# Attention block in one core: values copied by ScalarE without their bias, queries split by VectorE in another double step, and projections of values and outputs placed behind the values' products

## What is computed

```python
x = x + layernorm(attn(layernorm(x)))        # B, S, D, H, HD = 2, 2048, 128, 16, 64
x = x + layernorm(ffn(layernorm(x)))

def attn(x, Wq, bq, Wk, bk, Wv, bv, Wo, bo):
    q = einsum('bsd,dhk->bshk', x, Wq) + bq
    k = einsum('bsd,dhk->bshk', x, Wk) + bk
    v = einsum('bsd,dhk->bshk', x, Wv) + bv
    p = softmax(einsum('bqhd,bkhd->bhqk', q / sqrt(64), k))
    return einsum('bqhd,hdm->bqm', einsum('bhqk,bkhd->bqhd', p, v), Wo) + bo
```

## Time and profile before

| | |
|---|---|
| median of 3 runs | 2389.18 us (2385.74 to 2389.94) |
| profiled execution, time | 2388.58 us |
| profiled execution, span | 2386.7 us |
| mean granted TensorE clock over the span | 0.992 |
| PE busy | 98% of the span |
| DVE busy | 2035.4 us, 85% |
| POOL busy | 2107.2 us, 88% |
| ACT busy | 1415.4 us, 59% |
| DMA | mean 26 GB/s |

### The profile page before, as it was taken

The page is one execution under the profiler, slowest core; times in us unless marked ns, Lnnn a source line. Parts: engine busy times, 40 slices in busy tenths (PEclk is TensorE's granted clock), DMA queues, the critical chain, the costliest instruction groups (busy, mean ns, idle before and its releaser), DMA issues.

```text
span 2386.7 us, 43553 instructions
## 1 busy us (share of the span) xinstructions
PE 2348.6 (98%) x15628; PEld 1178.0 (49%) x15628; DVE 2035.4 (85%) x3208; ACT 1415.4 (59%) x1671; POOL 2107.2 (88%) x1206
## 2 busy tenths in 40 slices
PE   6999999999999999999999999999999999999998
PEld 3455454545445454454545445454544545444454
DVE  7888888888888888888888888888888888888877
ACT  5656556566565656656565655656656565655646
POOL 5888989888898989989888898989989888899986
PEclk8999999999999999999999999999999999999999
DMA  1100001000000000100001000100000000110101
GB/s 51 29 14 28 28 15 33 28 15 28 28 20 28 28 15 28 34 15 27 28 16 32 28 19 23 33 23 20 28 27 20 28 28 15 35 30 21 37 27 36
DMA packets 62969, 62.55 MB, mean 26 GB/s; under 512 B 28868, under 2 KB 46660, under 8 KB 62756
## 3 DMA queue, kind: packets, MB, share of 16 engines
q1 hardware_dynamic: 61748, 59.44, 8.5%
q10 hardware_dynamic: 1008, 0.33, 0.1%
HBM read 56.88 MB, written 2.61 MB: 25 GB/s over the span
## 4 chain that ended last, share of the span: by engine, by line
PE 94%; DVE 2%; POOL 1%; DMA 1%; ACT 1%; issue 1%; SPq 0%; POOLq 0%; DVEq 0%; ACTq 0%
PE o_ps L442 37%; PE spare_ps L401 14%; PE score_ps L421 10%; PE score_ps L427 10%; PE score_ps L424 10%; PE spare_ps L387 3%; PE spare_ps L487 3%; PE spare_ps L378 3%; PE spare_ps L369 3%; PE spare_ps L454 1%; DVE max_part L867 1%; POOL total L1142 1%; DMA m_all<-m_scratch 0%; DVE ln_stats L835 0%; PE spare_ps L467 0%
## 5 line engine op out<-in xcount | busy, mean ns | idle before, releaser
L1142 POOL TENSOR_TENSOR total<-total,probs 128x832 f32<-128x832 f32 (+1 forms) x896 | 1761.0, 1965 | 232.6 <-ACT probs L691 161.1
L867 DVE TENSOR_REDUCE max_part<-spare_ps 128x1 f32<-128x512 f32 x2027 | 1303.6, 685 | 295.3 <-PE spare_ps L401 276.7
L691 ACT ACTIVATE probs<-score_ps 128x1024 f32<-128x1024 f32 x1024 | 999.2, 1021 | 785.4 <-PE score_ps L427 784.2
L442 PE MATMUL o_ps<-probs,v_sb 128*64 128x512 f32 x4096 | 977.2, 598 | 0.0
L442 PEld LDWEIGHTS o_ps<-probs,v_sb 128*64 128x64 f32 x4096 | 268.3, 136 | 434.7 <-issue 282.5
L401 PE MATMUL spare_ps<-k_hi,q_hi 64*128 64x512 f32 x2027 | 466.2, 454 | 6.9 <-DVE max_part L867 3.2
L401 PEld LDWEIGHTS spare_ps<-k_hi,q_hi 64*128 64x128 f32 x2027 | 195.2, 184 | 436.8 <-issue 262.1
L421 PE MATMUL score_ps<-q_hi,kd_hi 64*128 64x512 f32 x2048 | 406.9, 393 | 0.9 <-ACT score_ps L681 0.9
L427 PE MATMUL score_ps<-q_hi,kd_lo 64*128 64x512 f32 x2048 | 405.2, 392 | 0.0
L424 PE MATMUL score_ps<-q_lo,kd_hi 64*128 64x512 f32 x2048 | 403.8, 390 | 0.0
L903 DVE TENSOR_REDUCE part_sum<-probs 128x192 f32<-128x768 f32 (+1 forms) x255 | 392.4, 1539 | 0.8 <-ACT probs L691 0.7
(11 more groups left out here) (136 smaller groups left out, 1118.5 us busy)
## 6 DMA issues: line engine op xcount, KB each, us to landing
m_all<-m_scratch SPq DMA_DIRECT2D x64, 512.0 KB, 4.4
denom<-denom_scratch SPq DMA_DIRECT2D x122, 128.0 KB, 2.9
m_scratch<-neg_rows SPq DMA_DIRECT2D x256, 1.0 KB
y_acc<-in_L_attn_x SPq DMA_DIRECT2D x8, 256.0 KB, 6.6
key_f<-in_L_attn_x SPq DMA_DIRECT2D x8, 256.0 KB, 2.8
block_out<-probs SPq DMA_DIRECT2D x8, 256.0 KB, 2.3
denom_col<-denom SPq DMA_DIRECT2D x61, 4.0 KB
denom_scratch<-denom_col SPq DMA_DIRECT2D x61, 4.0 KB, 1.4
```

The source lines that it names most:

```text
L442: last = nc.tensor.matmul(o_ps[half(h), :], v_sb[:, b, kt, half(h)], probs[:, st % RING, h, :], start=(kt == 0), stop=(kt == T - 1))
L691: nc.scalar.activation(probs[:, st % RING], score_ps[st % 2][:], ACT.Exp, scale=SCALE).then_inc(s["exp_done"], 1)
L867: nc.vector.reduce_max(max_part[:, G % 2, h, qt, kc:kc + 1], bank[max_bank(n, h)], AX.X).then_inc(s["max_done"], 1)
L1142: nc.gpsimd.tensor_tensor(others(total[:, G % 2], G), so_far, others(probs[:, st % RING], G), ALU.add).then_inc(s["sum_done"], 1)
```

## The change

The copy of the values moves from VectorE to ScalarE and loses its bias (`act_v`). The bias goes into the output's bias before the loop: `pool_bias` multiplies all of Wo with bv and folds the eight pairs together, `bias` lets TensorE sum over the rows at n = 3, and `dve_bias` adds that to `bo`. V runs in four groups of four tiles at d = 5 of every quarter. Q runs at d = 7, one quarter earlier than before counted in quarters (G + 3 instead of G + 2), and VectorE makes both of its parts. On TensorE V and Wo stand behind the values' products; Q and K stay ahead of them. On VectorE the output's addition stands behind the partial sums.

```diff
-V_AT = {(0, 7): (0, 2), (1, 7): (2, 2), (2, 4): (4, 2), (2, 7): (6, 2), (3, 0): (8, 3), (3, 4): (11, 3), (3, 7): (14, 2)}
+V_AT = {(0, 5): (0, 4), (1, 5): (4, 4), (2, 5): (8, 4), (3, 5): (12, 4)}
-Q_AT, M_OUT_AT, M_BACK_AT = 2, 4, 5
+Q_AT, M_OUT_AT, M_BACK_AT = 7, 4, 5
+def queries_at(n):
+    if n == 2:
+        return 2
+    G = n // PER_CHUNK + 3
+    return G if n % PER_CHUNK == Q_AT and G < CHUNKS else None
+BIAS_AT = 3
-FIRST_V_AT = {(2, 7): (0, 4), (3, 0): (4, 4), (3, 4): (8, 4), (3, 7): (12, 4)}
+FIRST_V_AT = {(1, 5): (0, 4), (2, 5): (4, 4), (3, 4): (8, 4), (3, 6): (12, 4)}
+            def bias(self):
+                self.pe.wait_ge(s["bias_scaled"], 4)
+                ps = self.take(SPARE["bias",], "bias", 0)
+                for k in range(2):
+                    last = nc.tensor.matmul(ps[half(k), 0:D], ones[:], bias_rows[:, 0, :], start=True, stop=True)
+                last.then_inc(s["bias_ps"], 1)
 # TensorE's loop
                 if keys_at(u, c, d):
                     me.project_k(*keys_at(u, c, d))
-                if values_at(u, c, d):
-                    me.project_v(*values_at(u, c, d))
-                if d == Q_AT and G + 2 < CHUNKS:
-                    me.project_q(G + 2)
-                if projected_at(G, d) is not None:
-                    me.out_projection(projected_at(G, d))
+                if queries_at(n):
+                    me.project_q(queries_at(n))
...
                     me.values(2 * n - 2)
                     me.values(2 * n - 1)
+                if values_at(u, c, d):
+                    me.project_v(*values_at(u, c, d))
+                if projected_at(G, d) is not None:
+                    me.out_projection(projected_at(G, d))
 # ScalarE
+        def act_v(act, u, t0, nt, name=None):
+            at = u * T + t0
+            act.wait_ge(s["v_ps"], at + nt)
...
+            nc.scalar.activation(v_sb[:, u % B, t0:t0 + nt, :].rearrange("p t n -> p (t n)"), bank[name or SPARE["V", at]][:, 0:nt * P],
+                                 ACT.Copy).then_inc(s["v_done"], nt)
...
                     act_seed(act, 2 * n + 3)
+                if values_at(u, c, d):
+                    act_v(act, *values_at(u, c, d))
                 if keys_at(u, c, d):
                     act_k(act, *keys_at(u, c, d))
...
-                if d == Q_AT and G + 2 < CHUNKS:
-                    act_q(act, G + 2)
 # VectorE
         def dve_q(dve, G, name=None):
             ps = bank[name or SPARE["Q", G]]
+            dve.wait_ge(s["q_ps"], G + 1)
...
+            nc.vector.tensor_scalar(q_hi[:, G % Q_RING, :], ps, b_qk[:, G // (B * NC) % 2, 0:1], None, ALU.add).then_inc(s["q_hi_done"], 1)
             dve.wait_ge(s["q_hi_done"], G + 1)
...
-                if values_at(u, c, d):
-                    dve_v(dve, *values_at(u, c, d))
-                if projected_at(G, d) is not None:
-                    dve_y(dve, projected_at(G, d))
...
                     dve_merge(dve, G - 1)
+                if projected_at(G, d) is not None:
+                    dve_y(dve, projected_at(G, d))
 # GpSimd, once before the loop
+        def pool_bias(pool):
+            pool.wait_ge(s["bias_in"], 32)
+            nc.gpsimd.tensor_tensor(bias_rows, bias_rows, b_v[:].unsqueeze(2).to_broadcast([P, PAIRS, D]), ALU.mult).then_inc(s["bias_scaled"], 1)
+            for k, count in enumerate((4, 2, 1)):
...
```

More of the change, by code:

```diff
@@ L133, in spare_banks @@
             use("V", v * T + t0)
-        if d == Q_AT and G + 2 < CHUNKS:
-            use("Q", G + 2)
+        if queries_at(n):
+            use("Q", queries_at(n))
         if projected_at(G, d) is not None:
             use("Wo", projected_at(G, d))
+        if n == BIAS_AT:
+            use("bias")
         if n in HEADS_AT:
@@ L170, in build @@
     bk_v = bk.rearrange("(i h) k -> i (h k)", h=2)
-    bv_v = bv.rearrange("(i h) k -> i (h k)", h=2)
+    bv_v = bv.rearrange("(i h) k -> (h k) i", h=2)
+    wo_rows = Wo.rearrange("(i h) k m -> (h k) i m", h=2)
     ctx = ExitStack()
@@ L186, in build @@
         b_qk = sb("b_qk", [P, 2, 2])
[L187 removed]
+        b_v = sb("b_v", [P, PAIRS])
         w_o = sb("w_o", [P, 2, D])
@@ L350, in take @@
                     pe.wait_ge(s["exp_done"], k + 1)
+                elif was == "bias":
+                    pe.wait_ge(s["bias_done"], 1)
                 elif was == "U":
@@ L581, in pe_program @@
                     me.project_k(*keys_at(u, c, d))
-                if values_at(u, c, d):
-                    me.project_v(*values_at(u, c, d))
-                if d == Q_AT and G + 2 < CHUNKS:
-                    me.project_q(G + 2)
-                if projected_at(G, d) is not None:
-                    me.out_projection(projected_at(G, d))
+                if queries_at(n):
+                    me.project_q(queries_at(n))
                 if n in HEADS_AT:
                     me.head_projections(HEADS_AT[n])
+                if n == BIAS_AT:
+                    me.bias()
                 if n == CENTRE_AT:
@@ L661, in act_k_high @@
             nc.scalar.activation(kd_hi[:, u % B, c * CH:(c + 1) * CH], key_diff[:], ACT.Copy).then_inc(s["kd_hi_done"], 1)
+        def act_v(act, u, t0, nt, name=None):
+            at = u * T + t0
+            act.wait_ge(s["v_ps"], at + nt)
+            if u >= 2 and t0 == 0:
+                act.wait_ge(s["pv_done"], (u - 1) * NC * T)
+            nc.scalar.activation(v_sb[:, u % B, t0:t0 + nt, :].rearrange("p t n -> p (t n)"), bank[name or SPARE["V", at]][:, 0:nt * P],
+                                 ACT.Copy).then_inc(s["v_done"], nt)
         def act_q(act, G, name=None):
@@ L773, in act_program @@
             act_x(act, 4)
+            act_v(act, 0, 0, TC, FIRST_V_BANK)
             act_x(act, 5)
@@ L851, in dve_x_statistics, with dve_bias @@
             statistics(dve, [y_acc[:, g * TC + t, :] for t in range(TC)], g, s["stats_done"], s["mv_done"], g)
[L853 to L860, removed]
+        def dve_bias(dve):
+            dve.wait_ge(s["bo_in"], 16)
+            dve.wait_ge(s["bias_ps"], 1)
+            nc.vector.tensor_tensor(bo_sb[:], bank[SPARE["bias",]][:, 0:D], bo_sb[:], ALU.add).then_inc(s["bias_done"], 1)
         def dve_max(dve, n, h):
@@ L1083, in dve_program @@
                     dve_merge(dve, G - 1)
+                if projected_at(G, d) is not None:
+                    dve_y(dve, projected_at(G, d))
                 if keys_at(u, c, d):
                     dve_k(dve, *keys_at(u, c, d))
-                if d == Q_AT and G + 2 < CHUNKS:
-                    dve_q(dve, G + 2)
+                if queries_at(n):
+                    dve_q(dve, queries_at(n))
                 if n in HEADS_AT:
@@ L1244, in pool_program @@
             first_rstd(7)
+            pool_bias(pool)
             for n in range(DOUBLES):
@@ L1316, in sp_denom_back @@
                 sp.wait_ge(s["o_norm_done"], G - 1)
+            elif G == 0:
+                sp.wait_ge(s["bias_ps"], 1)
             for h in range(2):
```

23 lines of the change are left out of this document (14 added, 9 removed).

## The result

| | before | after |
|---|---|---|
| median | 2386.57 us (20 runs, 2384.91 to 2389.94) | 2391.18 us (20 runs, 2390.02 to 2392.83) |
| profiled execution, span | 2386.7 us | 2389.9 us |
| granted TensorE clock | 0.992 | 0.993 |
| PE, DVE, ACT, POOL busy | 98%, 85%, 59%, 88% | 98%, 86%, 59%, 88% |

The ratio is 1.0017, 95% interval 1.0011 to 1.0023: the changed kernel is 0.17% slower, inside the 0.2% that was called no change. The time forecast was 2391, worked out from a median before of 2389.18 over three runs; over twenty runs that median is 2386.57. The change forecast was +2.3 us; the change measured is +4.6.

What follows compares the result with a forecast made beforehand. TensorE, busy 98%, was taken as the bound. +2.4 us steady and one-time terms made +2.3 on the profiled 2388.58, so 2390.9, forecast as 2391 with the median 0.6 above; range 2377 to 2404, chance 0.44 of staying within 4.8 us.

Steps and rivals of the forecast that it cites:

- +2.4 in the steady part: Sum of the quarter's terms, +0.04 us a quarter, over some 60 quarters.
- -0.1 once: One-time terms outside the steady quarters: bias matmuls 0.2 us, and -0.3 for VectorE's dropped first copy of values.
- d = 5 and 6: V's move to d = 5 costs 0 within 0.02; d = 6 loses its 0.12 us from late VectorE.
- d = 7: Q ahead of the products still waits 0.16 us for VectorE, where V waited 0.15.
- d = 2: VectorE starts pair A's reductions 0.85 late after the output's addition; costs 0.06 us, between 0 and 0.12.
- d = 3: The merge makes VectorE reduce pair A 0.88 late; costs 0.09 us, between 0 and 0.12.
- Placing V and Wo behind the products: At d = 5 and d = 1 on TensorE: V's place priced at 0, moving Wo gains nothing.
- rival 2: Slower: output's addition bounds d = 2, from a delay of 0.95; 18 us, 2409; chance 0.28 including its half.
- rival 1: Faster: VectorE on time at d = 7, 2372, chance 0.12; only d = 2 and 3 free, 2382, chance 0.16.
- All that the change can win in the steady part: TensorE's loss to late VectorE at d = 6 and 7: about 0.27 us a quarter, 17 us in 64 quarters.
- The bias's matmuls: One-time cost of TensorE's four passes of 128 columns for the folded bias: 0.2 us.
- The start, -0.3: VectorE's first copy of values leaves a stretch where TensorE waits for it: between 0 and -0.7 us.

Runs made afterwards that it cites:

- experiment 6: Changed kernel with V and Wo back ahead of the products, nothing else: 2390.22 us, ratio 1.0012.
- Experiment 4: Changed kernel with the output's addition back ahead of the partial sum and the merge on VectorE, Wo still behind the products: 2474.94 us.
- experiment 10: Changed kernel, V at d = 7, Q at d = 2 with ScalarE's Q part first, n = 2 banks in TensorE's order, `v_split` at n = 480: 2382.34 us.
- experiments 1 and 2: First: kernel before with V in fours at d = 5, 2403.82 us; second: changed kernel with Q at d = 2, high part on ScalarE, 2408.82 us.
- experiment 3: Changed kernel with the spare banks of n = 2 handed out in TensorE's order, Q before V: 2390.92 us, ratio 1.0016.
- Experiment 9: Changed kernel with n = 2 banks in TensorE's order and VectorE's `v_split` made at n = 480: 2388.96 us, ratio 1.0005.
- experiment 8: Changed kernel with n = 2 banks in TensorE's order and the last Q at n = 486 instead of 487: 2390.75 us, ratio 1.0013.
- experiment 1: Kernel before with V in groups of four at d = 5, still copied by VectorE and ahead of the products: 2403.82 us, ratio 1.0072.
- experiment 5: Changed kernel with n = 2 banks in TensorE's order, V at d = 7, Q at d = 2 with high part on ScalarE: 2387.57 us, ratio 1.0002.

## Why the prediction was right, and where it was wrong

**The time was right in part by chance.** Forecast were +2.4 in the steady part and -0.1 once, on a base of 2389.18. The base was 2.6 too high and the change by the medians, +4.6, twice what was forecast; the two errors cancel to the 2391. The profile shows +0.11 a unit, which is +0.03 a quarter for the +0.04 forecast and 1.4 us in units 1 to 13, and +1.7 at the ends. The steady part bears the forecast out, though in part by luck as well: d = 6 gave 0.04 less and d = 2 cost 0.06 less than forecast, and these cancel. The ends don't: they held two things that the prediction hadn't looked for.

**d = 5 and 6** (0 and -0.12): right in kind. 4.79 and 3.92 us. In this quarter d = 6 gave the 0.12; on the mean of a unit it was 4.00 before, because of the 3.97 in the third quarter, and gave 0.08.

**d = 7** (Q waits 0.16): right. 4.96 is 3.92 + 0.88 + 0.16. VectorE's first operation for Q has a pitch of 0.77 (1260.86 to 1261.63), where 0.66 was taken between 0.60 and 0.75: above the upper bound by 0.02, and covered as forecast, since the next pair A is still reduced 0.54 behind TensorE (1262.89 in the same timeline, against 1262.35). The Trainium skill, "VectorE: DVE Perf Modes", section on the TRN2 errata, gives an estimate of 0.66; the 62 operations here have a mean duration of 0.74.

**d = 2** (0.06, between 0 and 0.12): the term was mis-sized, it is 0. TensorE's timeline and VectorE's at d = 1 to 3 of a quarter after:

```profile
1232.31 0.39 PE L419 MATMUL spare_ps<-k_hi,q_hi 64*128 64x512 f32 x2
1232.63 1.94 PE L460 MATMUL o_ps<-probs,v_sb 128*64 128x512 f32 x8
1234.40 1.04 PE L505 MATMUL spare_ps<-w_o,o_sb 128*64 128x128 f32 x16
1235.37 0.50 PE L419 MATMUL spare_ps<-k_hi,q_hi 64*128 64x512 f32 x2
...
1239.31 0.51 PE L419 MATMUL spare_ps<-k_hi,q_hi 64*128 64x512 f32 x2
```

```profile
1233.95 1.52 DVE L938 TENSOR_REDUCE part_sum<-probs 128x192 f32<-128x768 f32 x1
1235.49 0.69 DVE L981 TENSOR_TENSOR y_acc<-spare_ps,y_acc 128x512 f32<-128x512 f32 x1
1236.10 1.28 DVE L898 TENSOR_REDUCE max_part<-spare_ps 128x1 f32<-128x512 f32 x2
...
1238.76 1.51 DVE L947 TENSOR_REDUCE total<-part_sum 128x192 f32<-128x768 f32 x1
1240.20 2.65 DVE L898 TENSOR_REDUCE max_part<-spare_ps 128x1 f32<-128x512 f32 x4
```

The addition starts 1.09 behind Wo, 0.04 sooner than K's copy starts behind K, and Wo starts 2.09 behind pair B where 2.18 was taken. Both together bring VectorE to 0.73 behind pair A where 0.85 was forecast. So much is early enough: experiment 6 has 0.60 and the same time. **d = 3** (0.09): right, 0.10, with VectorE 0.89 behind pair A. The Trainium skill's rule that weight loads are pulled ahead of running matmuls ("TensorE: Matmul & The Clock Gate", "Step-by-step: what each phase is for") would have made this free; the trace shows a price of 0.10 at 0.89 and none at 0.73.

**Placing V and Wo behind the products** (nothing, either way): right by experiment 6. Experiment 4 shows that this holds because the addition moved with Wo: with the addition back in its old place rival 2's mechanism comes about, and costs 84 us.

**The rivals.** Half of rival 1's cheaper form came true, d = 2 free; the other half, d = 3, didn't, and Q's wait stayed. Rival 2's delay of 0.95 at d = 2 was not reached (0.73).

**"All that the change can win in the steady part", 17 us:** the sum didn't rest on this step, and no run won that much: the best, experiment 10, won 0.30 a unit, under 5 us. What the step left out is that time at d = 7 also covers the seeds, with a margin of 0.21. V's wait of 0.15 fits into that margin; the 0.50 that V's tiles take at d = 7 doesn't. The waits before showed nothing of this, for the margin was still positive. The expectations of experiments 1 and 2 carried the omission further: they took d = 7 to 4.02, were forecast faster, and lost 0.40 to 0.45 at d = 0.

**Once.** The bias's matmuls, 0.2: right, n = 3 takes 4.15 for 3.92. The start, -0.3: -0.85, but this can't be credited to the change. Ahead of the loop and into n = 0, TensorE was granted the lower clock for 20.5 us in the profile before and for 13.7 in the one after; experiment 6, whose program is the changed kernel's up to there, shows 20.5 us and starts the loop 0.7 later than it. No run shows the term by itself. Not foreseen: +1.8 at n = 2 by the order in which banks are handed out, shown by experiment 3, and +2.0 at n = 488. Experiment 9 shows that this hangs on the wait behind the split; why the clock falls after it in some kernels and not in others is open. n = 0 gave back 0.7, which goes with the clock too (4.61 us after, 5.53 in experiment 6), and in the last unit one Q fewer gave back 0.75 and other places 0.3. The first unit holds that Q instead; n = 8 and 16, together 0.9 shorter, made up for it.

## What to carry to other kernels

A wait that a profile shows may be hiding a second one that it doesn't: before shortening a double step, add up what every engine must do in it (here ScalarE's four operations) and read the margin at which the next consumer starts. When an order of work is moved in one engine's program, look at everything that was derived from the old order: the hand-out of buffers and the queues of the engines that read the result; a mismatch in a single double step cost more than 50 quarters of the steady change. When two edits come together, run each without the other: V's move without Q's was 0.7% slower, which nothing in the 0.2% of both gave away. And a forecast of a time is two forecasts, of the base and of the change; look at the change.

## What the runs showed of the hardware

- TensorE's clock was granted in full after waits of 1.71 and 2.29 us in the kernel before and experiment 1, and fell to 1.2 GHz for some 3.4 us after waits of 1.67 and 2.15 us at the same double step in experiment 8 and the changed kernel. In that stretch four transposes took 0.93 and 1.12 us for 0.66. Each is one profiled execution.
- The same VectorE operation on 32 x 512 with both inputs in SBUF (`v_split`) took from 0.79 us (experiment 10) to 2.18 us (experiment 4). In all thirteen profiles a GpSimd operation on SBUF was running when it began, and it ended 0.55 us behind the end of that operation.
- ScalarE's copy of 128 x 512 out of PSUM took 0.60 us on the mean of 64 in the changed kernel; VectorE's copy of the same values with the bias added took 0.68 on the mean of 64 in experiment 1. No double step of the steady quarters shows a wait of TensorE for ScalarE's copy; n = 2 of experiment 5, where Q's part was queued behind it, does (2.21 us).
